# Four PSUM banks for the scores, three for the maximum chunks, in a fused AdaLN attention and expert layer

## The reference, cut to what matters

```python
# B=4 batches, S=2048 tokens, D=256, H=16 heads of dk=16; 8 experts, top 2
h = layernorm(x) * (1 + ca) + sa
Q, K, V = einsum('bsm,qhdm->qbhsd', h, W_qkv)
scores = where(causal_mask, -1e30, Q @ K.T) / sqrt(dk)
attn = softmax(scores, axis=-1)                 # exp(s - rowmax) / sum
x = x + ga * (concat_heads(attn @ V) @ W_o.T)
h = layernorm(x) * (1 + cb) + sb
x = x + gb * moe(h)                             # relu(h W1)^2 W2, weighted by the router
```

## Time and profile before

| what | us |
|---|---|
| runs of the kernel before | 3319.33, 3322.39, 3322.65 (median 3322.39) |
| the profiled execution, whole | 3324.03 |
| its span, first to last instruction | 3322.0 |
| PE busy | 3105.5 (93% of the span) |
| DVE busy | 2682.4 (81%) |
| ACT busy | 1825.9 (55%) |

### The profile page before, as it was taken

The page is one execution under the profiler, slowest core; times in us unless marked ns, Lnnn a source line. Parts: engine busy times, 40 slices in busy tenths (PEclk is TensorE's granted clock), DMA queues, the critical chain, the costliest instruction groups (busy, mean ns, idle before and its releaser), DMA issues. The chain is left out here.

```text
span 3322.0 us, 74403 instructions
## 1 busy us (share of the span) xinstructions
PE 3105.5 (93%) x19792; PEld 1828.5 (55%) x19792; DVE 2682.4 (81%) x6211; ACT 1825.9 (55%) x3693; POOL 385.1 (12%) x306
## 2 busy tenths in 40 slices
PE   6859999999999999999999995899999999999998
PEld 5741333333333333333333322798888888888887
DVE  6969888887888888888889822888888888888885
ACT  3640676776767676667667775444444343444343
POOL 1230000000000000000000000122223222222223
PEclk8985999999999999999999998899999999999999
DMA  4881222012211221022211003100000010000000
GB/s 157 288 257 37 62 62 62 19 56 63 66 29 41 67 62 46 28 63 62 63 32 42 15 11 98 37 26 27 27 27 26 29 47 30 27 27 26 27 14 14
DMA packets 138103, 182.55 MB, mean 55 GB/s; under 512 B 14544, under 2 KB 99792, under 8 KB 137680
## 3 DMA queue, kind: packets, MB, share of 16 engines
q1 hardware_dynamic: 129232, 169.14, 16.7%
q10 hardware_dynamic: 8448, 8.39, 0.8%
HBM read 109.59 MB, written 67.11 MB: 53 GB/s over the span
## 5 line engine op out<-in xcount | busy, mean ns | idle before, releaser
L706 ACT ACTIVATE probs<-ps 128x512 f32<-128x512 f32 (+3 forms) x2560 | 1173.4, 539 | 610.6 <-PE ps L800 365.8
L735 DVE TENSOR_REDUCE early<-ps 128x1 f32<-128x512 f32 x1536 | 1003.2, 686 | 130.3 <-PE ps L778 111.6
L778 PE MATMUL ps<-ks,qs 96*128 96x512 bf16 (+3 forms) x2560 | 887.9, 364 | 58.2 <-POOL ks L684 30.6
L796 PE MATMUL ps<-qs,ks 99*128 99x512 bf16 (+3 forms) x2560 | 831.1, 351 | 29.4 <-ACT probs L706 18.8
L778 PEld LDWEIGHTS ps<-ks,qs 96*128 96x128 bf16 x2560 | 247.7, 98 | 643.5 <-DVE early L735 233.5
L813 PE MATMUL ps<-probs,vs 128*32 128x512 f32 (+3 forms) x5120 | 600.8, 541 | 0.0
L731 DVE CUSTOM_DVE_ANT_0 junk<-ps,causal 128x128 bf16<-128x128 f32 (+3 forms) x1024 | 488.4, 485 | 78.6 <-PE ps L778 65.1
L1345 PE MATMUL ps<-w_hi,hid_hi 128*128 128x256 f32 x1536 | 438.4, 285 | 12.0 <-DVE mix L1222 6.0
L1348 PE MATMUL ps<-w_hi,hid_lo 128*128 128x256 f32 x1536 | 431.7, 281 | 0.0
L1347 PE MATMUL ps<-w_lo,hid_hi 128*128 128x256 f32 x1536 | 431.3, 281 | 0.0
L796 PEld LDWEIGHTS ps<-qs,ks 99*128 99x128 bf16 x2560 | 246.9, 98 | 326.8 <-ACT probs L706 194.5
(11 more groups left out here) (121 smaller groups left out, 3275.3 us busy)
## 6 DMA issues: line engine op xcount, KB each, us to landing
v_ones<-vt SPq DMA_DIRECT2D x16, 1024.0 KB, 6.4
vs<-v_ones SPq DMA_DIRECT2D x16, 1024.0 KB, 6.8
contexts<-ctx_out SPq DMA_DIRECT2D x64, 256.0 KB, 2.2
q_parts<-parts SPq DMA_DIRECT2D x32, 384.0 KB, 3.8
k_parts<-parts SPq DMA_DIRECT2D x32, 384.0 KB, 4.6
qs<-q_parts SPq DMA_DIRECT2D x64, 192.0 KB, 3.0
ks<-k_parts SPq DMA_DIRECT2D x64, 192.0 KB, 3.5
xin<-in_x ACTq DMA_DIRECT2D x16, 512.0 KB, 4.1
```

Source lines behind the costliest of these rows:

```text
L706: nc.scalar.activation(probs[u % PB][:, h, q0:TB], bank(n % SB)[:, q0:TB], ACT.Exp, scale=SCALE).then_inc(exp_done[p], 1)
L735: nc.vector.tensor_reduce(early[:, h, t, k0 // CW:k0 // CW + 1], tile, AX.X, ALU.max).then_inc(max_done[p], 1)
L778: mm = nc.tensor.matmul(bank(4 + c % MS * (CW // 512), CW // 512)[:, m0:m0 + n], qs[p][0:STACK, h, t * P:(t + 1) * P], ks[p][0:STACK, h, k ...
L796: mm = nc.tensor.matmul(bank(n % SB)[:, q0:TB], ks[p][:, h, kt * P:(kt + 1) * P], qs[p][:, h, j * TB + q0:(j + 1) * TB], start=True, stop= ...
```

## The change

`SB` goes from 3 to 4 and `MS` from 4 to 3. Scores rotate over banks 0 to 3, so that head h always uses bank h. The chunks start at bank 4 as before and rotate over 4, 5 and 6. The context accumulator moves from bank 3 to bank 7, for `p_v` and for `context`. No instruction is added or removed; the constants of two waits change with `SB` and `MS`: score n waits for exp n - 4 in place of n - 3, chunk c for the reduction of chunk c - 3 in place of c - 4.

```diff
-SB = 3
+SB = 4
-MS = 4
+MS = 3
@@ context, on ACT
-                    nc.scalar.activation(ctx_out[j % 2][:, :], bank(3), ACT.Copy).then_inc(ctx_done[p], 1)
+                    nc.scalar.activation(ctx_out[j % 2][:, :], bank(7), ACT.Copy).then_inc(ctx_done[p], 1)
@@ p_v, on PE
-                        mm = nc.tensor.matmul(bank(3)[VW * h:VW * (h + 1), q0:TB], vs[p][:, kt, h, :],
+                        mm = nc.tensor.matmul(bank(7)[VW * h:VW * (h + 1), q0:TB], vs[p][:, kt, h, :],
```

## The result

The changed kernel takes 3369.18 us (median of 4 runs, 3366.6 to 3370.39) against 3321.18 for the kernel before (4 runs, 3319.33 to 3322.65): ratio 1.0144, 95% interval 1.0126 to 1.0161. It is slower by 48 us; 3368 was forecast.

A forecast was written before the change was run, and what follows sets the result against it. PE's order and stream were taken to set the time. Chunks +75, scores -20 and last group -9 gave +46 us on the profiled 3324.0: 3370.0 there, 3368 as a median, range 3328 to 3402.

The forecast's parts named there:

- The loader's 422 and 194 us of waits: Waits view before the change: PE's weight loader waiting for DVE (422) and ACT (194), not to be taken at its word.
- Chunks, +75: 15 groups, chunk banks four to three: 32 waits and 5.0 us a group with delays carried, 75 us added.
- the full sum (149): Rival for the 15 groups: all chunk shortfalls add, 9.9 us a group, 149 us in all, 3442; chance 0.08.
- the single largest shortfall per stretch of DVE (55): Lower bound for chunks: only the largest shortfall in each DVE stretch without a pause counts, 3.7 us a group, 55 in all.
- Scores, -20 in the 15 groups: Score banks three to four: 11 late score starts, 1.3 us a group, all vanish, 20 us saved.
- Last group, -9: Group without chunks: 24 full units save 0.33 us each, 8 us, plus 1 for the diagonal ones.
- the bound of 16: Upper bound on the last group's gain: ACT without a pause, 90.0 - 73.8 = 16 us.
- The 2.07 us for four exps: Last group: ACT's time for four exps, to which a unit of 2.40 us would fall with one more score bank.
- The stretch ahead of the scores, 0 to 3: 160 chunks before the first scores, DVE the slower side: put down as 0, at most 3 us.
- The forecast's own bounds: Stated as 55 to 100 us for chunks, 9 to 16 last group, 0 to 20 scores: 3340 to 3400.
- Clock rival: One stretch of lowered PE clock in every group adds 26 us on top of +46: 3394; chance 0.08.
- Hidden short waits: Faster rival: chunk waits of 0.16 us free in PE's array fill, leaving 27 us in all, 3313; chance 0.10.

## Why the prediction was right

- *Where to look.* The loader's 422 and 194 us of waits were set aside for the pace of starts. The loader's waits on DVE rose by 216 us (638 in all) while the block grew by 43, so a sum from that view would have been wrong by a large factor.
- *Chunks, +75.* Measured alone +77; 32 waits a group forecast, about 36 counted (534 in all). The delays of one chunk relieve the next: the full sum (149) was the rival of 3442, and the single largest shortfall per stretch of DVE (55) too little.
- *Scores, -20 in the 15 groups.* -21.2 with chunks on three banks in both kernels. Of the 19 score waits left, 17 are in the last group, as foreseen.
- *Last group, -9.* It gave -13.9, inside the bound of 16. The 24 full units were sized well: 8 us forecast, 8.6 measured by the distances between the units' first scores. The 16 diagonal units, put at 1 us, gave 5.3: two neighbours there, for instance, went from 2.35 and 2.14 to 1.99 and 1.78 us. The 2.07 us for four exps was also taken from a stretch in which ACT still waited for PE; saturated, 11 of them took 5.46 us:
```profile
2039.72 5.46 ACT L706 ACTIVATE probs<-ps 128x512 f32<-128x512 f32 x11
```
  That is 1.99 us for four, and full units in a row now take 1.97 in place of 2.40. But the full units just behind a diagonal gain only 0.15 to 0.48 us, on average 0.28, which brings the sum back near the 8 forecast.
- *The stretch ahead of the scores, 0 to 3.* +1.7 us, at clock 0.50 before and after, as DVE stays the slower side there.
- The groups with chunks were to be near 110.9 us and are 111.0 (1664.4/15). The last group gave 5 us more than forecast; this is made up by the 1.7 us ahead of the scores, the 1.9 behind the block, which the change doesn't touch and no run explains, and 1.7 in the groups (56.7 for 75 - 20 = 55). So part of the closeness of 3368 to 3369.18 is luck.
- *Range.* The forecast's own bounds, added as stated, give 3341 (55 - 20 - 16) to 3413 (100 - 0 - 9), not 3340 to 3400, and no row gives the 100. The upper end was thus drawn too low; the result doesn't come near it.
- *Clock rival.* The 15 groups' clock stayed at 0.99.
- *Hidden short waits.* The last chunk shown in the earlier trace rows, forecast 0.16 us late (its rows give 0.18), starts at 1100.64 in place of 1100.48, although the waits are far shorter than a matmul's record:
```profile
1100.26 0.38 PE L796 MATMUL ps<-qs,ks 99*128 99x512 bf16 x1
1100.64 0.39 PE L778 MATMUL ps<-ks,qs 96*128 96x512 bf16 x1
```

## What to carry to other kernels

Buffers split between two consumers of one producer are worth what the waits on each cost the producer's stream; read these from the distances between its starts, not from idle time of a loader that runs ahead. To price one buffer less, lay the end of the consumer's work n - (depth - 1) beside each start of n and carry the delay along; from four chunk banks to three this came within 3 us of 77, from three score banks to two it gave 252 where 221 were measured. A consumer that is idle much of the time is no proof that the buffers suffice: the round trip of a single item can be longer than the time until its buffer is wanted again. Where a stage needs only one of the two pools, give it the other's idle buffers there, before taking one away for the whole run.

## What was not expected

- With DVE's work halved the fourth chunk bank still mattered, ahead of the scores: PE's granted clock there was 0.64 with four banks and 0.50 with three, and the stretch 8 us longer. A PE that waits more ran at the lower clock, which makes its round trip longer; which came first the runs don't tell.
- In one of three groups, the first of each pass through DVE's loop, DVE began its first masked reduction about 2.9 us after its last work, though its chunk had long been there ([2.88 <-issue] in the changed kernel). Chunk 3 pays for this with three banks and chunk 4 with four. What DVE did in it the profile doesn't show.
